# Attention projections in three split terms: one raw input buffer, values projected two groups apart from before, residual moved from group 6 to group 1

## The reference, cut to what matters

```python
Q, K, V = (proj(Wq, bq), proj(Wk, bk), proj(Wv, bv))      # x @ W.T + b, 16 heads of 16
scores = einsum('bhqd,bhkd->bhqk', Q, K) * scale
...
out = where(use_sparse, sparse_out, dense_out)
x = x + out @ Wo.T + bo                                    # then three more layers
```

## Time and profile before

| | |
|---|---|
| median of 3 executions | 1984.78 us (1984.0 to 1987.01) |
| the profiled execution, its own time | 1988.33 us |
| span of its trace | 1986.4 us |
| granted TensorE clock over the span | 0.969 of full |
| TensorE matmul, busy | 1839.2 us (93%) |
| VectorE, busy | 1485.8 us (75%) |
| ScalarE, busy | 1180.6 us (59%) |
| GpSimd, busy | 664.7 us (33%) |

### The profile page before, as it was taken

How to read it: one execution, slowest core, us unless ns; L and a number is a source line. 1 busy time by engine, 2 the same in 40 slices (tenths; PEclk the granted TensorE clock), 3 DMA queues, 4 the chain that set the end, 5 groups by cost and what they waited for, 6 DMA issues and landing times. The chain is left out here.

```text
span 1986.4 us, 43323 instructions
## 1 busy us (share of the span) xinstructions
PE 1839.2 (93%) x14542; PEld 1452.8 (73%) x14542; DVE 1485.8 (75%) x2206; ACT 1180.6 (59%) x2458; POOL 664.7 (33%) x655
## 2 busy tenths in 40 slices
PE   5899999999999994499999999999949999999997
PEld 4565555555555552388888888888849999999997
DVE  6888888888888892787878777787736666666664
ACT  1676667666666662366666666666545555555563
POOL 3244444444444442433343434333301111111111
PEclk9999999999999996699999999999979999999998
DMA  3333333333333320100000000000022222222221
GB/s 94 102 125 105 114 116 123 110 109 118 118 119 106 112 94 27 30 1 0 0 0 0 0 0 0 0 0 0 0 91 62 71 71 82 85 71 71 79 88 46
DMA packets 104940, 126.16 MB, mean 64 GB/s; under 512 B 27840, under 2 KB 70464, under 8 KB 104896
## 3 DMA queue, kind: packets, MB, share of 16 engines
q1 hardware_dynamic: 86912, 102.72, 16.3%
q0 software_dynamic: 17408, 22.61, 3.8%
q10 hardware_dynamic: 576, 0.26, 0.1%
HBM read 56.54 MB, written 9.44 MB: 33 GB/s over the span
## 5 line engine op out<-in xcount | busy, mean ns | idle before, releaser
L409 DVE TENSOR_REDUCE a_top<-a_s 128x4 f32<-128x1024 f32 x256 | 309.1, 1209 | 88.5 <-PE a_s L646 88.4
L509 ACT ACTIVATE a_e<-a_t 128x512 f32<-128x512 f32 x512 | 276.6, 592 | 147.7 <-PE a_t L660 143.2
L419 DVE SCALAR_TENSOR_TENSOR a_e<-a_e,a_w_t 128x1024 f32<-128x1024 f32 x256 | 328.1, 1282 | 6.3 <-ACT a_e L509 6.3
L1733 ACT ACTIVATE c_hid<-c_pH,c_b 128x256 f32<-128x256 f32 x256 | 107.4, 471 | 190.1 <-PE c_pH L1796 189.7
L926 POOL TENSOR_TENSOR b_decayed<-b_table,b_mod_t 128x1024 f32<-128x1024 f32 x64 | 118.8, 1876 | 211.3 <-ACT b_mod_t L1198 211.3
L1357 PE MATMUL b_pS<-b_gated_t,b_decayed 128*128 128x256 f32 x768 | 183.8, 389 | 1.0
L675 PE MATMUL a_v<-a_e,a_v_pad 128*32 128x256 f32 x2048 | 165.4, 396 | 8.8 <-DVE a_e L419 6.9
L641 PE MATMUL a_s<-a_absent,a_eye 64*128 64x512 bf16 x1024 | 157.1, 386 | 6.7 <-DMA a_absent<-a_absent 5.4
L1796 PE MATMUL c_pH<-c_x_hi,c_w_hi 128*128 128x256 f32 x512 | 150.8, 294 | 12.5 <-DVE c_w_lo L1698 12.4
L1357 PEld LDWEIGHTS b_pS<-b_gated_t,b_decayed 128*128 128x128 f32 x768 | 142.3, 192 | 23.8 <-issue 6.7
L646 PE MATMUL a_s<-a_st 63*128 63x256 f32 x1024 | 152.5, 377 | 0.0
(11 more groups left out here) (253 smaller groups left out, 5152.3 us busy)
## 6 DMA issues: line engine op xcount, KB each, us to landing
a_st<-a_split SPq DMA_DIRECT2D x384, 128.0 KB, 2.2
a_xs<-in_xT SPq DMA_DIRECT2D x32, 256.0 KB, 2.7
x_all<-in_xT SPq DMA_DIRECT2D x32, 256.0 KB, 3.6
a_r_rep<-a_r_rows POOLq DMA_DIRECT2D x64, 128.0 KB, 3.7
c_we<-in_we SPq DMA_DIRECT2D x32, 256.0 KB, 2.7
c_key_t<-in_keyT SPq DMA_DIRECT2D x32, 256.0 KB, 3.2
c_value<-in_key SPq DMA_DIRECT2D x32, 256.0 KB, 2.7
out<-c_y POOLq DMA_DIRECT2D x32, 256.0 KB, 3.3
```

The costliest lines, as they stand in the source:

```text
L409: dve.tensor_reduce(top[:, qc, half].rearrange("p (r j c) -> p r j c", r=2, j=2)[:, :, cc], ps_s[g % 2][:], AX.X, ALU.max)\
L419: dve.scalar_tensor_tensor(out=buf[:], in0=buf[:], scalar=BIG, in1=w_t[par][:, kc].unsqueeze(1).to_broadcast([P, 4, S]), op0=ALU.min, op1= ...
L509: act.activation(e[g % E_BUFS][:, 2 * r:2 * r + 2], ps_t[r][:], ACT.Exp).then_inc(exp_done, 1)
L1733: ins = act.activation(hid[r % 2][:, i], pH[r][:, i], ACT.Gelu, bias=b1[:, 2 * r + i:2 * r + i + 1])
```

## The change

The three projections are computed as three products of float32r parts: high weight with high x, low weight with high x, high weight with low x. The high parts of the weights are made once by ScalarE, the low parts once by GpSimd. For every batch ScalarE rounds x to `xs_hi` (`high_xs`, group 5) and GpSimd subtracts it from x to get `xs_lo` (`low_xs`, group 6). There is one raw buffer `xs` in place of two; its next load waits for `xs_lo_done`. The raw weights lie in `raw_v`, which isn't in use yet at that time. `project_v` moves from groups 3 and 4 to 2 and 3, ScalarE's `values` from 4 to 3, GpSimd's `residual` from group 6 to group 1. In `body` of SP the load of x moves ahead of `stack(n + 2, par, 0)`.

```diff
-    xs = [sb(f"xs{i}", [P, C, S], F32) for i in range(2)]
+    xs = sb("xs", [P, C, S], F32)
+    xs_hi = [sb(f"xs_hi{i}", [P, C, S], F32R) for i in range(2)]
+    xs_lo = [sb(f"xs_lo{i}", [P, C, S], F32R) for i in range(2)]
...
+    wq, wk, wv = raw_v[0][0], raw_v[0][1], raw_v[1][0]
...
+        def staged(n):
+            sp.wait_ge(xs_lo_done, n)
+            sp.dma_start(xs[:], ...).then_inc(d_xs, 16)
+        staged(1)
+        staged(2)
         stack(0, 0, 0)
...
+            if stage:
+                staged(n + 3)
             if proj:
                 stack(n + 2, par, 0)
             if maxi:
                 place_max(n + 1, 1 - par, 0)
-            if stage:
-                staged(n + 3, 1 - par)
...
+        def low_weight(i, low, w, high):
+            pool.wait_ge(scaled, 3 + i)
+            pool.tensor_tensor(low[:], w[:], high[:].bitcast(F32), ALU.subtract).then_inc(w_lo_done, 1)
+        def low_xs(n, par):
+            pool.wait_ge(xs_hi_done, n + 1)
+            pool.tensor_tensor(xs_lo[par][:], xs[:], xs_hi[par][:].bitcast(F32), ALU.subtract).then_inc(xs_lo_done, 1)
...
             if finish:
                 denominators(n - 1, 1 - par, 0)
+            if not (isinstance(n, int) and n < 3):
+                after_weigh(n, 1)
+                residual(n - 3)
...
-            if not (isinstance(n, int) and n < 3):
+            if stage:
                 after_weigh(n, 6)
-                residual(n - 3)
+                low_xs(n + 3, 1 - par)
...
+        low_weight(0, wq_lo, wq, wq_hi)
+        low_xs(0, 0)
+        low_weight(1, wk_lo, wk, wk_hi)
+        low_xs(1, 1)
+        low_weight(2, wv_lo, wv, wv_hi)
...
+        def high_xs(n, par):
+            act.wait_ge(d_xs, 16 * (n + 1))
+            if not (isinstance(n, int) and n < 2):
+                act.wait_ge(proj_v, n - 1)
+            act.activation(xs_hi[par][:], xs[:], ACT.Copy).then_inc(xs_hi_done, 1)
...
-                if g == 4 and maxi:
+                if g == 3 and maxi:
                     values(n + 1, 1 - par)
+                if g == 5 and stage:
+                    high_xs(n + 3, 1 - par)
...
         def project_q(n, par):
-            pe.wait_ge(d_xs[par], landed(n, par))
+            pe.wait_ge(xs_lo_done, n + 1)
...
+            product(n, par, wq_lo, wq_hi).then_inc(proj_q, 1)
+        def product(n, par, w_lo, w_hi):
+            terms = [(a, b, k) for k in range(C) for a, b in ((w_hi, xs_hi[par]), (w_lo, xs_hi[par]), (w_hi, xs_lo[par]))]
             for m in range(C):
-                for k in range(C):
-                    ins = pe.matmul(bank[:, m], wq[:, k, m * P:m * P + P], xs[par][:, k], start=(k == 0), stop=(k == C - 1))
-            ins.then_inc(proj_q, 1)
+                for i, (a, b, k) in enumerate(terms):
+                    ins = pe.matmul(bank[:, m], a[:, k, m * P:m * P + P], b[:, k], start=(i == 0), stop=(i == len(terms) - 1))
+            return ins
...
-                if maxi and g in (3, 4):
-                    project_v(n + 1, 1 - par, g - 3)
+                if maxi and g in (2, 3):
+                    project_v(n + 1, 1 - par, g - 2)
```

More of the change, by code:

```diff
@@ L65, in attention_layer @@
     ident, ident_bf, iota_bf = consts["ident"], consts["ident_bf"], consts["iota_bf"]
-    wq, wk, wv, wo = (sb(n, [P, C, D], F32) for n in ("wq", "wk", "wv", "wo"))
+    wq_lo, wk_lo, wv_lo = (sb(n + "_lo", [P, C, D], F32R) for n in ("wq", "wk", "wv"))
+    wq_hi, wk_hi, wv_hi = (sb(n + "_hi", [P, C, D], F32R) for n in ("wq", "wk", "wv"))
+    wo = sb("wo", [P, C, D], F32)
     bias = sb("bias", [P, 4, C], F32)
@@ L129, in attention_layer @@
     pool_seen = zero
+    w_lo_done, xs_hi_done, xs_lo_done = sem("w_lo"), sem("xs_hi"), sem("xs_lo")
     def batches(eng, body):
-        body(0, 0, True, True, False)
+        body(0, 0, True, True, True, False)
         for n in range(1, 4):
[L135 to L141, removed]
+            body(n, n % 2, True, True, True, True)
+        if NB > 8:
+            with pairs(eng, 4, NB - 4) as n:
+                body(n, 0, True, True, True, True)
+                body(n + 1, 1, True, True, True, True)
+        body(NB - 4, 0, True, True, True, True)
+        body(NB - 3, 1, False, True, True, True)
+        body(NB - 2, 0, False, False, True, True)
+        body(NB - 1, 1, False, False, False, True)
     STACK_DMAS = TERMS * 2
@@ L183, in place_max @@
             sp.dma_start(st[par][63::64, 0, 2 * half:2 * half + 2].bitcast(F32), max_row[half][:].bitcast(F32)).then_inc(d_max[half], 16)
+        def staged(n):
+            sp.wait_ge(xs_lo_done, n)
+            sp.dma_start(xs[:], t["xT"][bass.ds(n, 1)].rearrange("o (k p) s -> p (o k) s", p=P)
+                         if not isinstance(n, int) else t["xT"][n].rearrange("(k p) s -> p k s", p=P)).then_inc(d_xs, 16)
+        staged(1)
+        staged(2)
         stack(0, 0, 0)
@@ L188, in _ @@
         place_max(0, 0, 0)
[L190 to L194, removed]
         def body(n, par, stage, proj, maxi):
@@ L303, in spread, with body @@
                                r_rows[:, half].unsqueeze(1).to_broadcast([4, DH, C * S])).then_inc(d_rep, 16)
+        def low_weight(i, low, w, high):
[4 more added lines that the diff above has]
+            pool.tensor_tensor(xs_lo[par][:], xs[:], xs_hi[par][:].bitcast(F32), ALU.subtract).then_inc(xs_lo_done, 1)
         def after_weigh(n, g):
             at_least(pool, p_done, n * GROUPS + g)
-        def body(n, par, proj, maxi, finish):
+        def body(n, par, stage, proj, maxi, finish):
             if proj:
@@ L343, in _ @@
         masks(1, 1)
+        low_xs(2, 0)
         weights(0, 0)
@@ L464, in _ @@
         act.wait_ge(scaled, 2)
+        def high_xs(n, par):
[3 more added lines that the diff above has]
+            act.activation(xs_hi[par][:], xs[:], ACT.Copy).then_inc(xs_hi_done, 1)
+        act.activation(wq_hi[:], wq[:], ACT.Copy).then_inc(scaled, 1)
+        high_xs(0, 0)
+        for high, w in ((wk_hi, wk), (wv_hi, wv)):
+            act.activation(high[:], w[:], ACT.Copy).then_inc(scaled, 1)
         def whole_q(n):
@@ L569, in _ @@
             if n == 0:
+                high_xs(1, 1)
                 act.wait_ge(zero, 6)
@@ L573, in _ @@
         place_absent()
+        high_xs(2, 0)
         act.wait_ge(set_up, READY)
@@ L590, in project_q @@
                 pe.wait_ge(mrow_done[1], n - 1)
+            product(n, par, wq_lo, wq_hi).then_inc(proj_q, 1)
+        def product(n, par, w_lo, w_hi):
+            terms = [(a, b, k) for k in range(C) for a, b in ((w_hi, xs_hi[par]), (w_lo, xs_hi[par]), (w_hi, xs_lo[par]))]
             for m in range(C):
-                for k in range(C):
-                    ins = pe.matmul(bank[:, m], wq[:, k, m * P:m * P + P], xs[par][:, k], start=(k == 0), stop=(k == C - 1))
-            ins.then_inc(proj_q, 1)
+                for i, (a, b, k) in enumerate(terms):
+                    ins = pe.matmul(bank[:, m], a[:, k, m * P:m * P + P], b[:, k], start=(i == 0), stop=(i == len(terms) - 1))
+            return ins
         def project_k(n, par):
             pe.wait_ge(qf_done, C * (n + 1))
[L598 to L601, removed]
+            product(n, par, wk_lo, wk_hi).then_inc(proj_k, 1)
         def project_v(n, par, m):
@@ L609, in project_v @@
                     pe.wait_ge(kf_done, 1 if isinstance(n, int) and n == 0 else n + 2)
-            for k in range(C):
-                ins = pe.matmul(bank[:, m], xs[par][:, k, m * P:m * P + P], wv[:, k], start=(k == 0), stop=(k == C - 1))
+            terms = [(a, b, k) for k in range(C) for a, b in ((xs_hi[par], wv_hi), (xs_hi[par], wv_lo), (xs_lo[par], wv_hi))]
+            for i, (a, b, k) in enumerate(terms):
+                ins = pe.matmul(bank[:, m], a[:, k, m * P:m * P + P], b[:, k], start=(i == 0), stop=(i == len(terms) - 1))
             if m == C - 1:
```

10 lines of the change are left out of this document (5 added, 5 removed).

## The result

The changed kernel takes 1964.61 us as a median, against 1984.39 for the kernel before measured with it: a ratio of 0.9897 (95% interval 0.9883 to 0.9911), 19.8 us faster. The forecast was 1972, faster by 13, with a range of 1958 to 1985. The profiled execution has a span of 1963.5 us against 1986.4. In this change the values move by one group, from 3 and 4 to 2 and 3; the title's "two groups" is wrong.

What follows compares the result with a forecast made beforehand. TensorE, ScalarE and VectorE take turns on a batch's path. -0.41 - 0.30 + 0.22 = -0.49 us a batch, x 29 = -14.2, start +1.0: 1988.33 becomes 1975.1, as a median 1971.6; range 1958 to 1985.

Steps and rivals of the forecast that it cites:

- likeliest case: Whole kernel: gains and losses as summed, 1972 us, own range 1965 to 1979; chance 0.50.
- Three things take turns in a batch: Attention loop: the 22.35 us path of a batch alternates between TensorE, ScalarE and VectorE, so shorter products differ in worth.
- Prices of the split products: TensorE projections: 0.119 us per split product plus 0.20 change-over; q or k 1.63, a chunk of v 0.91.
- more is gained: Rival for the projections: split terms pay no change-over, -0.89 us a batch, 1959 us; chance 0.20.
- The residual's move, 0.41 a batch: From M (start of group 4's mix_values) to turn_max: no wait for the a_delta copy, gain 0.41 us a batch.
- the gain is absorbed: Rival: high_xs delays ScalarE's exps and a_delta copy, so turn_max waits as before; -0.08 us a batch, 1983.5 us; chance 0.18.
- q, nothing: q product: 0.26 us shorter, but project_k still waits for ScalarE's whole_q; worth 0 on the path.
- turn to k: From turn_max to project_k: 4.00 us a batch, claimed to be ScalarE's stretch, not TensorE's.
- k, 0.30 a batch: k product: all of its 0.30 us saving counts on the path of a batch (0.10 to 0.50).
- Values into groups 2 and 3, a loss of 0.22 a batch: VectorE's row maximum of group 3 starts 0.22 us later (0.02 to 0.42); group 4 has TensorE level again.
- high_xs and low_xs at nothing: Added ScalarE copy (0.71 us) and GpSimd subtraction (1.26 us) in each batch: cost 0 each.
- The start, +1: Before the loop: longer way to q(0), less shorter products and an earlier load, together +1 us (-1 to +5).

Runs made afterwards that it cites:

- r4: Changed kernel with the q product in two terms, the low weight's product left out: 1964.38 us, ratio 0.9893 to the kernel before.
- r5: Changed kernel with the k product in two terms, the low weight's product left out: 1946.99 us, ratio 0.9808 to the kernel before.
- r12: Changed kernel with residual back in group 6 ahead of low_xs and values back in groups 3 and 4: 1977.30 us, ratio 0.9970 to the kernel before.
- r2: Changed kernel with the residual back in group 6, ahead of low_xs: 1983.13 us, ratio 0.9985 to the kernel before.
- r1: Kernel before with only the residual moved from group 6 to group 1: 1971.77 us, ratio 0.9933 to the kernel before.
- r3: Changed kernel with the values projected in groups 3 and 4 again: 1962.02 us, ratio 0.9885 to the kernel before.
- r8: Changed kernel with one more GpSimd subtraction ahead of low_xs in group 6: 1990.97 us, ratio 1.0030 to the kernel before.
- r7: Changed kernel with low parts of the three weights and batch 0's x made by VectorE, not GpSimd: 1963.62 us, ratio 0.9887 to the kernel before.

## Why the prediction was right

Faster, by 19.8 us where 12.8 was forecast (1984.39 - 1971.6): inside the range of 1958 to 1985, and 0.4 below the lower end of the likeliest case's own, 1965 to 1979. By its steps:

- **Three things take turns in a batch, TensorE's time alone doesn't count.** Shown: 0.48 us of q is worth 0 (r4), 0.48 us of k is worth 0.46 (r5). The split without the moves saves 0.86 of TensorE's time and 0.24 of the batch (r12).
- **Prices of the split products**, 1.63, 1.63 and 0.91: measured 1.64, 1.63 and 0.91. The 0.20 us for changing over, taken from the f32 products, holds for split terms, and the case "more is gained" falls with it, though the time, 1964.6, lies nearer to its 1959 than to 1972. By the number alone the wrong case would have looked the better one.
- **The residual's move, 0.41 a batch.** The turn's wait is gone, and the stretch from M to the turn fell by 0.48: the rows of waits gave 0.41, a little too small a price. Undoing the move costs 0.56 (r2), 0.53 of it in this stretch. The move alone is worth 0.43 (r1). The case "the gain is absorbed" falls: high_xs is in, and the turn has no wait.
- **q, nothing.** Nearly right: 0.05 a batch. I had called turn to k ScalarE's stretch alone, but in the earlier trace rows TensorE has no slack in it either: q's start, 1.89 and 1.08 end at 324.34, where k begins. In every second batch whole_q started 3.11 after the turn, right behind the end of the f32 q, where it starts at 3.05 with the split q, and k came at 4.00 instead of 3.91. In the others it was 3.84 and 3.83. This is read from the rows of the kernel before, of r1 and of the changed kernel; no run changes the f32 q alone.
- **k, 0.30 a batch.** 1.93 to 1.63. Shown by the row and by r5.
- **Values into groups 2 and 3, a loss of 0.22 a batch: this term was mis-sized.** The 0.22 at group 3 is there to the hundredth, and at group 4 it comes again, where I had TensorE level. But I had left VectorE's stretch at 8.12 with its collisions in it, and the delay itself moves weigh 2 and 3 out of GpSimd's way, 0.33 less, so that this stretch fell by 0.14. Net cost 0.07 (r3). This is the largest part of the 0.24 us by which a batch came out shorter than forecast; the turn's 0.07 and q's 0.05 are the rest.
- **high_xs and low_xs at nothing.** low_xs as it stands costs nothing that shows; one subtraction more in its place costs 26 us (r8), so it has little room. I didn't test high_xs apart. The stretch from M to the turn, where the prediction feared it, is 4.23 on average with it (the changed kernel) and without it (r1).
- **The start, +1: mis-sized**, +3.0 in the profiled execution. I priced the longer way to q(0) and left out that GpSimd's subtractions run beside VectorE's one-hot rows, three beside the first run and four (low_part among them, since the second run ends later) beside the second, which stretches these by 3.3 and 4.2 us. The first stretch is hidden: that run ends at 20.17, and VectorE then waits 2.76 for TensorE. Of the second, r7 gives 1.7 us back. I had weighed such a collision for weigh and didn't look for it here. I also called q(0)'s slow products a lower clock. The rows show the pace (0.21 us a term after the change), but the granted clock is recorded as 1.00 from 14 to 21 us, so its cause stays open.

The two misses have opposite signs, -7.1 in the loop and +2.0 at the start by the spans. That they cancel in part is luck, and so is some of the time's nearness to the forecast: the loop alone gained 21.3 us where 14.2 was forecast.

## What to carry to other kernels

Walk one period of a software pipeline from the last wait back to itself and name the engine of every stretch; an engine that is 97% busy may still own only part of the path, and then the same 0.48 us is worth everything in one product and nothing in the next. When a step is moved, recompute the collisions of VectorE and GpSimd with the new start times: here two row maxima came 0.22 us late each, and the batch paid only 0.07, since the delay stepped around two collisions. And look for the instruction that an existing wait is really about: the larger gain here was the move of one GpSimd addition, and the split of the projections alone gave 7 us.

## What the runs showed of the hardware that was not expected

- A VectorE instruction with two inputs in SBUF and a GpSimd addition or subtraction that overlap in time don't share: the second one's record is longer by the overlap less 0.12 to 0.15 us, in six cases (excess 0.05, 0.17, 0.32, 0.49 on VectorE, 0.39 and 0.98 on GpSimd).
- VectorE's one-hot rows, bf16 with a scalar operand, are stretched as well: 32 of them from 6.35 to 9.61 us beside three GpSimd subtractions of 1.3 us each, and to 7.51 beside one (r7).
- A product in three split terms pays the same change-over as an f32 product when it stands between products of other tile shapes: 0.20 us beyond 12 x 0.119, and 0.20 beyond 6 x 0.119.
